# Second attention layer's projection as a function of its own: transposes and products in one turn, bias through TensorE, products kept by ScalarE, residual three turns behind

## The reference, cut to what matters

```python
h = jnp.maximum(_layernorm(x, axis=-1), 0.0)
x = x + _L2_gnn_ref(h, edge_index, W_src, attn_src, attn_dst, bias)
# inside:
h = (x @ W_src).reshape(n, H, C)
a_src = (h * attn_src[None]).sum(-1)
a_dst = (h * attn_dst[None]).sum(-1)
...
out = out.reshape(n, H * C) + bias
```

## Time and profile before

| what | us |
|---|---|
| median of 3 runs | 3662.82 |
| lowest and highest of them | 3661.37, 3671.05 |
| the profiled execution | 3684.87 |
| its span in the profile | 3683.2 |
| mean granted clock of TensorE in it | 0.794 |

### The profile page before, as it was taken

The page is one execution under the profiler, slowest core; times in us unless marked ns, Lnnn a source line. Parts: engine busy times, 40 slices in busy tenths (PEclk is TensorE's granted clock), DMA queues, the critical chain, the costliest instruction groups (busy, mean ns, idle before and its releaser), DMA issues. The chain is left out here.

```text
span 3683.2 us, 52863 instructions
## 1 busy us (share of the span) xinstructions
PE 2249.8 (61%) x12839; PEld 1786.9 (49%) x12839; DVE 2173.2 (59%) x7930; ACT 1669.2 (45%) x3697; POOL 2036.5 (55%) x2221
## 2 busy tenths in 40 slices
PE   2316899998999675446556655874553644545442
PEld 1303666766677564446445553553543533333332
DVE  5516998998999686433534636944558533443242
ACT  0016999999998485222322335832441122222100
POOL 3878765665573431468038336703550058888767
PEclk9998999999999877567757757985666667777665
DMA  2511132332331262754266284425330534343363
GB/s 80 170 41 30 44 98 85 101 99 86 99 98 41 81 181 75 195 131 122 60 183 175 60 229 109 116 82 145 93 79 15 160 90 98 85 99 84 58 184 93
DMA packets 592914, 382.51 MB, mean 104 GB/s; under 512 B 50669, under 2 KB 540622, under 8 KB 592266
## 3 DMA queue, kind: packets, MB, share of 16 engines
q1 hardware_dynamic: 537050, 338.44, 31.5%
q0 software_dynamic: 52800, 39.73, 6.1%
q10 hardware_dynamic: 2800, 1.28, 0.3%
HBM read 250.72 MB, written 153.32 MB: 110 GB/s over the span
## 5 line engine op out<-in xcount | busy, mean ns | idle before, releaser
L1290 POOL DMA_INDIRECT p_a<-t_d,k_map_ix x300 | 312.0, 1040 | 431.8 <-DMA p_a<-t_d 378.0
L830 POOL TENSOR_TENSOR a_rs<-a_ve,w_neg_half 128x16 f32<-128x16 f32 x113 | 330.4, 2924 | 241.7 <-DVE a_ve L766 210.5
L856 ACT ACTIVATE a_nr<-a_xb,a_nm,a_rs 128x128 f32<-128x128 f32 x882 | 371.8, 490 | 26.0 <-POOL a_nm L832 26.0
L1787 PE MATMUL c_pq<-layer_src,c_sel 128*128 (+1 forms) x1000 | 243.1, 421 | 163.4 <-ACT c_sel L1757 107.5
L918 PE MATMUL a_ps<-w_ident,a_nr 128*128 128x128 f32 x1568 | 246.4, 281 | 127.5 <-ACT a_ht L864 47.6
L926 PE MATMUL a_ps<-a_ht,w_aug 128*128 128x512 f32 x588 | 315.0, 621 | 2.3 <-DVE a_ht L733 2.3
L918 PEld LDWEIGHTS a_ps<-w_ident,a_nr 128*128 128x128 f32 x1568 | 180.8, 143 | 276.2 <-issue 243.9
L1787 PEld LDWEIGHTS c_pq<-layer_src,c_sel 128*128 128x128 f32 x1000 | 211.4, 299 | 195.4 <-issue 114.0
L1412 PE MATMUL p_pm<-w_aug,p_ht 128*128 128x130 f32 (+1 forms) x1600 | 290.3, 354 | 8.0 <-issue 3.9
L1412 PEld LDWEIGHTS p_pm<-w_aug,p_ht 128*128 128x128 f32 x1600 | 274.4, 260 | 21.3 <-ACT p_ht L1373 11.2
L733 DVE TENSOR_TENSOR a_ht<-a_ps,a_ht 128x512 f32<-128x512 f32 x294 | 203.0, 694 | 136.2 <-ACT a_ps L871 113.3
(11 more groups left out here) (351 smaller groups left out, 6176.1 us busy)
## 6 DMA issues: line engine op xcount, KB each, us to landing
c_a<-t_d SPq DMA_DIRECT2D x125, 256.0 KB
t_d<-c_a SPq DMA_DIRECT2D x125, 256.0 KB
t_s<-p_a SPq DMA_DIRECT2D x100, 256.0 KB
a_xa<-in_x SPq DMA_DIRECT2D x98, 256.0 KB
out<-a_xb SPq DMA_DIRECT2D x98, 256.0 KB, 2.1
p_a<-t_s SPq DMA_DIRECT2D x75, 256.0 KB
p_a<-t_d SPq DMA_DIRECT2D x75, 256.0 KB
t_acc<-q_zt SPq DMA_DIRECT2D x3, 2171.5 KB
```

What stands on the lines that cost most here:

```text
L830: nc.gpsimd.tensor_tensor(RS[:, z, :], VE[:, z, :], w["neg_half"][:, None, 0:J].to_broadcast([P, LNS, J]), ALU.pow).then_inc(s_rstd.sem, 1)
L856: last = nc.scalar.activation(NR[k][:, T.at(NORM[k], 2), cols(j)], normed_rows(T, k)[:, cols(j)], ACT.Identity, bias=NM[:, T.at(1, SHORT), ...
L1290: eng.indirect_dma_start(out=A[:, g, SRC, j, :], out_offset=None, in_=t[f"d{r}"], in_offset=bass.IndirectOffsetOnAxis(ap=k["map_ix"][:, b ...
L1787: last = nc.tensor.matmul(PS[g][:, j, :], SEL[:, g, j, :], keep["src"][:, bass.ds(number(b) * J + j, 1), 0:C].rearrange("p o c -> p (o c)" ...
```

## The change

The kind "normed" leaves `project`, and a new function `project_heads` takes its place in `layer2_at_edges`. The other kinds keep their code and order. In the new function loads, gathers, moments, normalisation, transposes and copies are as before, except that a load waits for the normalisation of the block that held the slot and no longer for its products. What differs:

- TensorE multiplies block n in the turn in which it transposes block n. Before each product a matmul of the identity with the bias row (`BR`, 144 columns, on every partition) starts the sum in PSUM, and the product adds to it.
- ScalarE copies block n in turn n and, between normalisation and copy, keeps the products of block n-1 with two copies of 128x576.
- VectorE keeps nothing; its residual is three turns behind.

```diff
-        project(nc, w, k, t, 4, HEADS, w["aug2"][:, :], w["bias_rows"][0][:, :], "normed", False, keep)
+        project_heads(nc, w, k, t, 4, keep)
...
+def project_heads(nc, w, k, t, r, keep):
...
+            def load(b):
+                g = b % RING
+                if b >= RING:
+                    eng.wait_ge(s_out[g], (uses(b) - 1) * 16)
+                    eng.wait_ge(s_normed[DST], b - RING + 1)
...
+            for b in range(BLOCKS):
+                eng.wait_ge(s_next, b + 1)
+                eng.dma_start(block_rows(t[f"s{r + 1}"], b), A[:, b % RING, SRC, :, :]).then_inc(s_out[b % RING], 16)
+                if b and b - 1 + RING < BLOCKS:
+                    load(b - 1 + RING)
...
+            def residual(b):
+                g = b % RING
+                eng.wait_ge(s_keep[SRC], b + 1)
+                there(eng, b)
+                v.tensor_tensor(A[:, g, SRC, :, :], A[:, g, SRC, :, :], keep["src"][:, b * J:(b + 1) * J, 0:C], ALU.add).then_inc(s_next, 1)
+
+            LAG = 3
+            for n in range(BLOCKS + LAG):
+                if n <= BLOCKS:
+                    if n < BLOCKS:
+                        there(eng, n)
+                    mo.turn(eng, lambda m: A[:, n % RING, m // J, m % J, :], n, BLOCKS - 1)
+                if 0 <= n - LAG:
+                    residual(n - LAG)
...
+            def hold(b):
+                for side, name in sides:
+                    eng.wait_ge(s_mm[side], b + 1)
+                    nc.scalar.activation(keep[name][:, b * J:(b + 1) * J, 0:CW], PM[side][:, :, 0:CW], ACT.Copy).then_inc(s_keep[side], 1)
+
+            for n in range(BLOCKS + 1):
+                if n < BLOCKS:
+                    apply(n)
+                if n:
+                    hold(n - 1)
+                if n < BLOCKS:
+                    copy(n)
...
+            eng.wait_ge(s_bias, 2)
...
+            def product(b):
+                for side in (SRC, DST):
+                    eng.wait_ge(s_ht, b * 2 + side + 1)
+                    if b:
+                        eng.wait_ge(s_keep[side], b)
+                    for j in range(J):
+                        nc.tensor.matmul(PM[side][:, j, 0:CW], w["ident"][:, :], BR[:, :], start=True, stop=False)
+                        last = nc.tensor.matmul(PM[side][:, j, 0:CW], HT[:, b % SHORT, side, cols(j)], w["aug2"][:, :], start=False, stop=True)
+                    last.then_inc(s_mm[side], 1)
+
+            for n in range(BLOCKS):
+                turn(n)
+                product(n)
```

More of the change, by code:

```diff
@@ L1214, in project @@
     CW = C + 2 * heads
-    first, normed = kind == "first", kind == "normed"
-    sigmoid, norm, overlay = not normed, kind != "plain", not first
+    first = kind == "first"
+    norm, overlay = first, not first
     RING, SHORT = 7, 3
@@ L1224, in project @@
         HT = sb("ht", [P, SHORT, 2, J * C])
-        NR = HT[:, :, :, :].rearrange("p g s (j c) -> p g s j c", j=J)
-        UP = sb("up", [P, SHORT, J, C]) if sigmoid else None
+        UP = sb("up", [P, SHORT, J, C])
         XS = sb("xs", [P, SHORT, J, C]) if plus_x else None
@@ L1329, in residual @@
             def residual(b):
[L1330 to L1334, removed]
+                g, grow = b % RING, UP[:, b % SHORT, :, :]
+                eng.wait_ge(s_sig, b + 1)
                 if plus_x:
@@ L1357, in apply @@
                 eng.wait_ge(mo.s_shift, b + 1)
-                if normed and b >= SHORT:
-                    eng.wait_ge(s_mm[DST], b - SHORT + 1)
                 for side in (SRC, DST):
@@ L1363, in apply @@
                         rows = A[:, g, side, j, :]
-                        last = nc.scalar.activation(NR[:, m, side, j, :] if normed else rows, rows, ACT.Identity if normed else ACT.Relu,
+                        last = nc.scalar.activation(rows, rows, ACT.Relu,
                                                     bias=mo.shift[:, m, n:n + 1], scale=mo.rstd[:, m, n:n + 1])
@@ L1373, in copy @@
                     nc.scalar.activation(HT[:, b % SHORT, side, :], PT[b % 2][side][:, :, :].rearrange("p j c -> p (j c)"),
-                                         ACT.Relu if normed else ACT.Copy).then_inc(s_ht, 1)
+                                         ACT.Copy).then_inc(s_ht, 1)
             def squash(b):
@@ L1387, in _ @@
                     copy(n - copies)
-                if sigmoid and 0 <= n - squashes:
+                if 0 <= n - squashes:
                     squash(n - squashes)
@@ L1401, in turn @@
                     for j in range(J):
-                        rows = NR[:, b % SHORT, side, j, :] if normed else A[:, b % RING, side, j, :]
-                        last = nc.tensor.transpose(PT[b % 2][side][:, j, :], rows, w["ident"][:, :])
+                        last = nc.tensor.transpose(PT[b % 2][side][:, j, :], A[:, b % RING, side, j, :], w["ident"][:, :])
                     last.then_inc(s_tp, 1)
```

83 lines of the change are left out of this document (added).

## The result

The changed kernel took 3606.62 us (median of four runs, 3601.41 to 3608.49); the kernel before took 3662.1 us beside it. The ratio is 0.9844, with a 95% interval of 0.9821 to 0.9867. Forecast were 3609 us and a range of 3595 to 3633. The profiled execution of the changed kernel took 3608.49 us, 2 us over its median; that of before (3684.87) lay some 23 us over its own, so spans of the two are not compared here, only the changed stage.

A forecast was written before the change was run, and what follows sets the result against it. Bound: a loop of waits from residual to statistics, 18.9 to 19.5 us, to span three turns instead of two. Turn 24 55 us earlier, drain 1 us longer: 54 us off the 3662.82 median gives 3609 us, range 3595 to 3633.

The forecast's parts named there:

- The loop and its span: Second layer's projection: residual, store, loads, gathers, statistics take 18.9 to 19.5 us, over three turns not two: 6.5 each.
- The fill: Start of the stage, bound by GpSimd's first 28 gathers; turn 7 was to begin at 2592.
- The drain: From turn 24 to the end of the last residual: 17.8 us before, taken as 1 us more after.
- the sum of 54 us: Whole gain forecast: turn 24 begins 55 us earlier, the drain takes 1 us more.
- The hold: ScalarE's new 128x576 copy from PSUM that keeps the products: 0.66 us, scaled from 0.582 for 128x512.
- ScalarE's turn: ScalarE's normalisations, two copies and two holds per turn: 5.6 us, with handovers 5.8, under the 6.5 us turn.
- TensorE's term and the clock: TensorE's turn: 5.5 us at the high clock, 10.3 at the low; granted clock taken as 1.00.
- the relations' row: First layer of another kind, same ring, residual three turns behind: TensorE busy 17.84 of 20 us, clock 1.00.
- Rival 2: TensorE's clock falls between bursts of products: a turn of 7.9 us, 30 us gained, 3633 us; chance 20%.
- Rival 1: GpSimd's gathers become the bound with landings of 2.68 us: turns of 5.98 us, 3597 us; chance 15%.
- Rivals 3 and 4: TensorE stays at 1.2 GHz, 3705 us (3%); ScalarE falls a turn behind, residual not earlier, 3663 us (3%).
- the bias operations on VectorE: VectorE's two operations adding bias and keeping products, some 0.75 us each: removing them saves nothing by itself.

The follow-up runs named there:

- e1: Changed kernel with only the residual put back to four turns behind; ratio 0.9978 to the kernel before, stage 242.2 us.
- e7: Kernel before with a ring of eight slots for seven in this stage and nothing of the change; ratio 0.9873, stage 190.7 us.
- e8: Changed kernel with eight ring slots and the residual four turns behind; ratio 0.9833 to the kernel before, stage 184.3 us.
- e10: Changed kernel, seven slots, GpSimd's memset between gathers cut to 64 columns; ratio 0.9815 to the kernel before, stage 176.3 us.
- e12: Changed kernel with eight ring slots and GpSimd's memset between gathers cut to 64 columns; 3594.62 us, ratio 0.9783 to the kernel before.
- e11: Changed kernel unchanged, measured again on another run's chip; 3610.03 us, ratio 0.9828 to the kernel before, stage 182.9 us.
- e4: Changed kernel with the bias matmuls removed and the bias left out; ratio 0.9864 to the kernel before, stage 183.6 us.
- e2: Changed kernel with VectorE adding the bias and keeping the product, no bias matmuls; ratio 0.984 to the kernel before, stage 185.6 us.
- e3: Kernel before with the residual three turns behind and VectorE's hold put before it; ratio 0.9879, stage 193.1 us.
- e6: Changed kernel with eight ring slots for seven; ratio 0.9907 to the kernel before, stage 213.2 us.
- e5: Changed kernel with each bias matmul issued twice; ratio 0.9965 to the kernel before, stage 222.0 us.

## Why the prediction was right

**The loop and its span** were the step that decided, and held: 16.18 us from residual to the statistics that it feeds was forecast to stay, and was 16.19 in the last round. Its inside shifted. The first gather came 7.70 us after the residual (6.95 before), and the landing of the fourth took 4.02 (4.75 before, 2678.42 to 2682.44). That 16.19 meets 16.18 is in part chance: over turns 7 to 24 this stretch took 14.3 to 16.2 us after, and 13.3 to 16.7 before. The turn was forecast at the upper end, 6.5, of 6.31 to 6.50, and was 6.33, the lower: the triples average 19.0 us and not 19.5. Over 17 turns this is 3 us. e1, e7 and e8 show that it is this loop that took the turn from 9.46 to near 6.3, and e10 that it still counts there.

**The fill** was the term mis-sized. I let turn 7 begin 56.5 us into the stage (2592 less 2535.53), with bounds of 54.6 to 56.7; it began at 53.96. Turns 1 to 7 ran at GpSimd's own distance (5.97 us a turn) and the landing was the short one: 39.0 us from turn 0 to turn 7, against 46.2 before. The long landing of 4.75, which I took because loads are under way, was not there yet.

**The drain** was forecast 1 us longer and was 0.9: 22.33 us from turn 24 to the next stage, against 21.43. The two waits of nearly 5 us for ScalarE's holds in it are that engine's turns: the residuals that wait start 5.65 and 5.41 us apart, near the 5.6 worked out.

So the sum of 54 us was 59.5 in the stage: 0.1 us lost ahead of turn 0, 7.3 gained in the fill (4.6 forecast), 53.2 in 17 turns (50.4 forecast), 0.9 lost in the drain. The stage is 5.5 us off its forecast and the program's time only 2.4 us. That the time came nearer is luck, since the medians differ by 4 us less than the two stages.

**The hold** was forecast at 0.66 us, scaled by the element; the group of lines after has it at 0.634 and 0.638:

```profile
L1535 ACT ACTIVATE layer_src<-p_pm 128x576 f32<-128x576 f32 x25 | 15.8, 634 | 2.3 <-PE p_pm L1565 2.3
L1535 ACT ACTIVATE layer_dst<-p_pm 128x576 f32<-128x576 f32 x24 | 15.3, 638 | 3.7 <-PE p_pm L1565 3.7
```

ScalarE's turn was forecast at 5.6 to 5.8 us. e12, where it is the fullest engine, shows 5.54 with handovers.

**TensorE's term and the clock.** 1.00 was forecast, by the relations' row, and came. Rival 2 needed the clock to fall between bursts; in the changed kernel it was never under 0.91 in the windows of 20 us between 2550 and 2690 (in e11 one such window, 2660 to 2680, had 0.84). e4 shows that it does fall, to 0.66 to 0.83, when the bias matmuls go. It also shows that this costs nothing at half the product work. The Trainium skill's section "Part 4: PE-mode transpose" of "TensorE: Matmul & The Clock Gate", by which transposes don't count as busy in the same way, is not contradicted by this: the runs of the new function with a mean clock under 0.80, e2 (0.76) and e4 (0.74), are the two whose matmuls other than transposes were halved. No run here varied the transposes alone.

**Rival 1**, GpSimd as the bound, came true for a part of the stage. In e11, the same kernel, its gathers run back to back from block 2 to block 20, and the first statistics of turns 7 and 17 are 59.58 us apart, 5.96 a turn, GpSimd's own pace:

```profile
2578.36 0.30 DVE L1184 BATCH_NORM_STATS2 p_mo_st<-p_a 128x6 f32<-128x128 f32 x1 [1.95 <-DMA p_a<-t_d,k_map_ix]
...
2637.94 0.29 DVE L1184 BATCH_NORM_STATS2 p_mo_st<-p_a 128x6 f32<-128x128 f32 x1 [1.91 <-DMA p_a<-t_d,k_map_ix]
```

The landings of turns 8 to 17 are the short ones of the rival, 2.5 to 2.8 us, and with them the loop fits into three turns of GpSimd's own pace, 17.9 us. The last seven turns then take 6.88 us each, with landings of up to 5.4. So the 6.33 of the kernel after and the 6.34 of e11 are means of two bounds, the gathers' 5.96 and the loop with its long landing; the prediction took the second for all turns and stood near the mean. **Rivals 3 and 4** did not come: the clock stood near 1.00, and no residual waited for its hold before the drain.

**The parts that cost or bring nothing.** That the bias operations on VectorE "lay in its wait for data" was right for the kernel before (e1: 1.2 us). Once the residual is three turns behind and they stand ahead of it, they count for little: 1.7 us of the stage between e2 and the kernel after. With the old order of products as well it is 9.2 (e3).

## What to carry to other kernels

Where a ring is refilled behind a late step, count the turns between that step and the turn that uses the refill. Here the refill behind residual b is that of block b + slots - 1, so they are slots less one less lag: 7 - 1 - 4 = 2 before, 7 - 1 - 3 = 3 after. The length of the chain divided by that number is the pace as long as no engine's own turn is longer, and either number can be changed; here one `7` to `8` gave most of what a new arrangement of four engines gave. Compute moved between engines brought little here beside that (e1 1.2 us, e2 1.7), and after the chain is spread further, the next bound has to be tried on the chip: with eight slots the same kernel was 29 us slower in the stage on one chip, and with eight slots and a shorter filler between gathers 17 us faster on another.

## What the runs showed that was not expected

- ScalarE can start an instruction late though its inputs are there: in the rows of e6 2.86 us after the product's end, in e5 once 6.2 us. In the rows of e1 and e6 these late starts follow one another 1.48 to 1.53 us apart, near the distance of GpSimd's gathers (1.49). They occur in e1, e2, e4, e5 and e6.
- GpSimd's memset between gathers took 0.17, 0.33 and 0.54 us for 64, 256 and 512 columns, and the gathers were 1.33, 1.49 and 1.70 us apart: the gather's 1.00 us, the memset and 0.16 us.
- A gather's landing was 2.63 us at turn 7 (fourth gather at 2572.16, statistics at 2574.79) and 4.02 at turn 24.
- In the kernel after, measured again in e11, GpSimd's own pace and the loop share the stage between them: turns of 5.96 us first, then long ones.
- With half of the product work gone the granted clock fell from near 1.00 to 0.66 to 0.83, and the stage's time did not change (e4).
